# A fused tokeniser, attention and FFN kernel: a new order of all engines, queries placed by a maximum over one value, a buffer of its own for normalised rows

## The chip, the cores and the metric

One core of a Trainium2 chip. The metric is the device time of one execution in microseconds, as a median over executions. A profile of one further execution is shown, with its own time.

The engines are TensorE (PE; its weight loads have a row kind of their own, PEld), VectorE (DVE), ScalarE (ACT), GpSimd (POOL) and SyncE (SP), which in this kernel issues every DMA. Each engine runs its own instructions strictly in the order in which they were written; semaphores couple the engines. So an instruction that waits holds up everything behind it on its engine.

## The reference

64 images of 3 x 224 x 224 and 64 texts of 77 rows of 256 values. In essence:

```python
h = concat([tokens(x), txt], axis=1)              # 196 patch rows + 77 text rows, 256 wide
h = h + attention(layernorm(h))
h = h + ffn(layernorm(h))

def tokens(img):   # 14 x 14 patches of 768 values
    p = layernorm(patches(img)) * g + b
    return layernorm(p @ W + b) * g + b

def attention(x):  # per token: 16 heads attend to each other over the reshaped projections
    Q, K, V = proj(Wq, bq), proj(Wk, bk), proj(Wv, bv)
    return softmax(Q @ K.T * scale) @ V, then @ Wo.T + bo

def ffn(x):        # x_prev is x shifted by one token
    xr, xk = mu_r * x + (1 - mu_r) * x_prev, mu_k * x + (1 - mu_k) * x_prev
    return sigmoid(xr @ W_r) * (square(relu(xk @ W_k)) @ W_v)
```

By the labels of the reference's sums, for each token the 16 heads attend to one another (blocks of 16 by 16), and the result is reshaped without moving axes back, so that a row that goes into `Wo` holds one head's values of 16 tokens. The kernel therefore needs queries, keys and values in another layout than the projections give, and the attention's result in another again; both ways go through DRAM.

## The kernel before

Four images of 273 rows make a **quad** of 1092 rows, which is cut into three **chunks** of 364 rows (tiles of 126, 126 and 112 rows). There are 16 quads, 48 chunks, and the program is fully unrolled. While one chunk is in attention, the FFN of the chunk before and the tokeniser of images to come run between its steps, so that a chunk passes through several slots of the schedule.

The steps of a chunk that this text speaks of, with their lines:

- `qkv` (PE, L1048, output 126x384): projections, six products. `qb` (DVE, L863) adds the bias into `qkvt`.
- `qkv_out` (SP, L520): three DMAs, one for each tile, write `qkvt` to DRAM.
- `qk_in` (SP, L526): one DMA brings queries and keys back in the other layout, into `qk`. It waits for all three `qkv_out`.
- `qplace` (DVE, L849): two instructions put the queries into the two halves of the block-diagonal operand `qx`. `kspread` (ACT, L943): four instructions spread the keys. Both wait for `qk_in`.
- `s` (PE, L1085): scores, in two parts; waits for both `qplace` and all four `kspread`. Then `mx`, `sub` (DVE, L758, L763), `exp` (ACT, L948), `pt` (PE, L1093, transposes), `ptc` (ACT, L955).
- `v_in` (SP, L536): eight DMAs bring the values. `av` (PE, L1106): weighted values; waits for all eight `v_in`.
- `rec`, `osb` (DVE, L771, L775): normalise. `o_out` (SP, L541): nine DMAs to DRAM, once both `osb` are done. `o_in` (SP, L551): four DMAs bring the rows of an earlier chunk back as `on`, when the `o_out` that hold its last rows have landed.
- `ont` (PE, L1162), `onh`, `onl` (ACT, DVE): transposed rows; `wo` (PE, L1048, output 126x256), `h2` (DVE, L877): output projection and residual. `z` (ACT, L1005): normalised rows for the FFN, `zt` (PE, L1176) their transposes; `d`, `mix`, `k`, `r`, `val`, `add` the FFN; `out` (SP, L558) the result.
- Of images: `load` (SP, L489), `xcols`, `x`, `tok` (PE, L1116 and L1128), `h`, and `hdma` (SP, L513): three or four DMAs that put an image's finished patch rows into `hc`, the input rows of the chunks; `txt` (SP, L502) does the same for the text rows.

The order of every engine comes from one table of numbers, `AT`: each step has a position for each of its instructions, and every engine walks through all positions of a quad in rising order (`due`). A chunk step repeats every 4000 positions, an image step every 3000, a quad is 12000. A second table, `BANK`, gives each PE product its PSUM bank; `turn` makes PE wait for the last reader of what lay in that bank before.

One **slot** below is the stretch of 4000 positions in which one chunk goes from `o_out` of the chunk before it to its own `o_out`. The three slots of a quad differ in the image work that lies in them. In the order before, the first has `load` and `txt`, the second `load`, the third a whole `hdma` between `qkv_out` and `o_in`.

`on` and `z` are one buffer before: `o_in` waits until the transposes of the last `z` are through (L547), and `z` waits until `ont` has read `on` (L1003).

```python
def due(q, step, kind, j):
    k, rest = divmod(step - AT[kind][j], PERIOD[kind])
    if rest == 0 and exists(q, k, COUNT[kind]):
        yield k
```

Of the kernel before, what the change touches and what calls it, by code (L numbers as in the profile page):

```python
# [24 lines left out]
E = 256  # L25
HEADS, HD = 16, 16
# [5 lines left out]
TT = 126  # L32
TILES = 3
# [19 lines left out]
AT = dict(load=[0], xcols=[1555, 1687, 1876], sq=[3679], ssq=[4380], sqm=[4077, 4754], x=[2492, 2687, 2748],
    xh=[2643, 2784, 3076], xl=[2770, 3010, 3345], tok=[3700, 4609], stat=[4791], statc=[4894], statr=[4924],
    rstd1=[5338], txt=[10699], yn=[5350, 5424], st2=[6383, 6410], mv2=[6419, 6940], rstd2=[7253], hg=[6806, 7654],
    h=[7672, 8038], hdma=[9674], st3=[12693, 12843, 12966], mv3=[12988, 13082, 13112], rstd3=[13465], xn=[13777,
    13786, 13828], xt=[14114, 14194], xnh=[14323, 14438], xnl=[14474, 14695], hb=[18602], qkv=[14883, 15394, 15694,
    15965, 16265, 16340], qb=[15239, 15458, 15899, 16234, 16393, 16469], qkv_out=[16549, 17104, 17527],
    qk_in=[17953], v_in=[19005], qplace=[19042, 19048], kspread=[19082, 19222, 19230, 19256], s=[19435, 19452],
    mx=[19468, 19506], sub=[19575, 19604], exp=[19700, 19706], pt=[19710, 19922], ptc=[19888, 19894, 20053, 20060],  # L60
    av=[20075, 20094], rec=[20283, 20307], osb=[20293, 20332], o_out=[21113], o_in=[25935], ont=[26318, 26698],
    onh=[26409, 26726], onl=[26493, 26925], wo=[27035, 27261, 27330], h2=[27208, 27323, 27365], st4=[27324, 27769,
    27817], mv4=[27846, 27877, 27887], rstd4=[27943], z=[28233, 28349, 28364], zt=[28392, 28600], carry=[25727],
    ztc=[28522, 28666], d=[28888, 29076], edge=[29095], mix=[29171, 29248, 29941, 30014], mixh=[29528, 29665, 31342,
    31470], mixl=[29606, 29733, 31580, 31687], k=[30028, 30810], kr=[30222, 31508], ksq=[31257, 31771], kah=[31535,
    32120], kal=[31919, 32670], r=[32810, 33005, 33263], rt=[32874, 33121, 33343], val=[33333, 33595, 34000],
    rv=[33400, 33604, 34202], add=[34577, 35013, 35159], out=[34624, 36139, 37049], sqh=[4192])

BANK = dict(x=[5, 1, 3], tok=[1, 3], stat=[5], yn=[7], xt=[2, 4], qkv=[4, 5, 4, 6, 0, 2], s=[0, 6], pt=[2, 0],
    av=[2, 5], ont=[6, 0], wo=[5, 0, 6], zt=[4, 6], k=[5, 2], r=[0, 5, 2], val=[0, 2, 0])  # L70
BANK_ORDER = ("s", "pt", "av", "x", "tok", "stat", "xt", "qkv", "ont", "wo", "zt", "k", "r", "val", "yn")

XCUT = [(0, 5), (5, 10), (10, 14)]
# [1 line left out]
             "yn", "st2", "mv2", "rstd2", "hg", "h", "hdma")  # L75
PERIOD = {kind: IMG if kind in IMAGE_OPS else SLOT for kind in AT}
COUNT = {kind: IPQ if kind in IMAGE_OPS else CPQ for kind in AT}
STEPS = sorted({(a + PERIOD[kind] * i) % QUAD for kind, at in AT.items() for a in at for i in range(COUNT[kind])})
# [9 lines left out]
def exists(q, k, count):  # L88
    return not isinstance(q, int) or 0 <= count * q + k < count * QUADS
# [97 lines left out]
def fusion_kernel(nc, x, txt, ln1_g, ln1_b, tok_w, tok_b, ln2_g, ln2_b, wq, bq, wk, bk, wv, bv, wo, bo,  # L187
                  w_r, w_k, w_v, mu_r, mu_k, out):
    with ExitStack() as ctx:
        def sb(name, shape, dt=F32):  # L190
            return ctx.enter_context(nc.sbuf_tensor(name, shape, dt))

        def sig(name, per, primed=False, unit=1):
            return Signal(ctx, nc, name, per, CPQ, primed, unit)

        def isig(name, per, primed=False, unit=1):
            return Signal(ctx, nc, name, per, IPQ, primed, unit)
# [16 lines left out]
        xcols = sb("xcols", [XROWS, GRID * 128])  # L214
# [3 lines left out]
        rstd1 = sb("rstd1", [PT, 2])  # L218
# [4 lines left out]
        mv2 = sb("mv2", [PT, 2, 2])  # L223
# [12 lines left out]
        qx = sb("qx", [128, GR, 2, HD])  # L236
        qk = sb("qk", [128, GR, 2 * HD])
# [6 lines left out]
        osb = probs  # L244

        mx = sb("mx", [128, BLK // 4 * 8])
        rsum = mx
        pt2 = sb("pt2", [128, BLK, 2, 2, HD])


        on = sb("on", [TT, TILES, E])
        z = on
        onT = sb("onT", [128, 2, 2, CT], F32R)
        zT = sb("zT", [128, 2, 1 + CT])

# [1 line left out]
        kr = dT  # L257
# [3 lines left out]
        r = sb("r", [TT, TILES, E])  # L261
# [20 lines left out]
        def settle(eng):  # L282
            eng.sem_inc(settled, 1)
# [25 lines left out]
        st3 = sig("st3", 3)  # L309
# [30 lines left out]
        st4 = sig("st4", 3)  # L340
# [3 lines left out]
        z_pe = sig("z_pe", 2, True)  # L344
# [103 lines left out]
        def _(sp):  # L448
# [33 lines left out]
            def body(q):  # L482
                for s in STEPS:
# [59 lines left out]
                    for k in due(q, s, "o_in", 0):  # L543
                        after_all(o_out, q, k)
                        if k % CPQ < 2:
                            after_all(o_out, q, k + 1)
                        after(z_pe, q, k - 1, 2)  # L547
                        after(on_pe, q, k - 1, 2)
                        for m, r0, rows, i, p in row_pieces(k % CPQ):
                            src = o_dram[m, :, :, :].rearrange("q t d -> (q t d)").rearrange("(r e) -> r e", e=E)  # L550
                            on_in.done(sp.dma_start(on[p:p + rows, i, :], src[r0:r0 + rows, :]))  # L551
# [152 lines left out]
        def _(dve):  # L704
            V = nc.vector
# [41 lines left out]
            def body(q):  # L747
                for s in STEPS:
                    for n in weights_due(q, s):
                        square_weight(n)  # L750
                    for part in range(PARTS):
# [14 lines left out]
                        val, total = rows[:, :, 0:4 * HD].rearrange("p t (y d) -> p t y d", y=4), rows[:, :, 4 * HD:AVW]  # L766
# [76 lines left out]
                    for xx in range(2):  # L843
                        for k in due(q, s, "qplace", xx):
                            qk_in.wait(dve, q, k, 1)
                            s_pe.wait(dve, q, k - 1, PARTS)
                            settle(dve)
                            half = slice(64 * xx, 64 * xx + 64)
                            q_sb.done(V.tensor_copy(qx[half, :, xx, :], qk[half, :, 0:HD]))  # L849
                    for kk in range(2):  # L850
                        for k in due(q, s, "xnl", kk):
                            xn_hi.wait(dve, q, k, kk + 1)
# [53 lines left out]
        def _(act):  # L906
# [27 lines left out]
            def body(q):  # L934
                for s in STEPS:
# [64 lines left out]
                    for i, (o, rows) in enumerate(TOK):  # L1000
                        for k in due(q, s, "z", i):
                            rs4_pool.wait(act, q, k, 4)
                            on_pe.wait(act, q, k, 2)  # L1003
                            z_pe.wait(act, q, k - 1, 2)
                            z_sb.done(A.activation(z[0:rows, i, :], h2[0:rows, k % CPQ, i, :], ACT.Identity,  # L1005
                                                   bias=nm4[0:rows, i:i + 1], scale=rs4[0:rows, i:i + 1]))
# [212 lines left out]
```

How the kernel before makes its waits and increments, by code:

```python
    def wait(self, eng, q, k, steps):  # L162
        eng.wait_ge(self.sem, q * (self.count * self.per) + (self.base + k * self.per + steps * self.unit))
# [1 line left out]
    def done(self, ins):  # L165
        ins.then_inc(self.sem, self.unit)
        return ins
# [9 lines left out]
    def wait(self, eng, q, k):  # L177
        back, i = divmod(k, len(self.pers))
        eng.wait_ge(self.sems[i], q * self.pers[i] + (2 + back) * self.pers[i] + self.pers[i])
# [279 lines left out]
            def load_rest():  # L460
# [4 lines left out]
                        sp.dma_start(dst, v.rearrange("(a e) -> a e", a=1).broadcast_to((128, E))).then_inc(raw_in, 16)  # L465
                    for n, w in enumerate(WEIGHTS):
                        sp.dma_start(rawsq[n], w.rearrange("(a p) e -> p a e", p=128)).then_inc(raw_in, 16)
                    for s, v in ((0, mu_k), (1, mu_r)):
                        sp.dma_start(mus[:, s, :], v.rearrange("(k p) -> p k", p=128)).then_inc(raw_in, 16)
                sp.wait_ge(prep_pool, 1)
                for c in range(CPQ):
                    sp.dma_start(qkv_dram[c, CT:CTP, :, :].rearrange("t i j -> t (i j)"), qkvt[0:CTP - CT, 0, :]).then_inc(raw_in, 16)
# [9 lines left out]
            def body(q):  # L482
# [10 lines left out]
                    for k in due(q, s, "txt", 0):  # L493
                        back, m = divmod(k, IPQ)
                        c = back * CPQ + text_pieces(m)[-1][2]
                        if q * IPQ + k == 0:
                            sp.wait_ge(prep_act, ACT_CLEAR)
                        after(xn_sb, q, c - CPQ, 3)
                        after(hb_sb, q, c - CPQ, 1)
```

## Time and profile before

| what | value |
|---|---|
| median of 3 runs | 1629.72 us (1624.85 to 1634.03) |
| the profiled execution | 1621.5 us, span 1619.8 us |
| busy: PE, PEld | 1451.5 us (90%), 1383.3 us (85%) |
| busy: DVE, ACT, POOL | 1203.4 us (74%), 1107.2 us (68%), 1023.6 us (63%) |
| busy of the 16 DMA engines | 77.3% by the queue that SP issues on |
| granted PE clock, mean | 0.965 |

Busy times say what an engine had to do; whether it was waited for shows only in the views of waits and in the timeline. A row of the timeline is one or several instructions of a line that follow one another: start, length, engine and line, what is written from what, how many, and in brackets the idle time ahead of it with what ended it. A row of waits is engine and line, what it waited for, and then the sum, the count and the longest. SPq is SP's queue of instructions: the length of a DMA row there is how long SP took to issue it, not how long the transfer took.

### The profile page before, as it was taken

The page shows a single profiled execution, that of the slowest core. Times are in us where ns is not written, and L with a number is a line of the kernel's source. Part 1 is how long each engine was busy: PE and PEld are TensorE (multiplying, and loading weights), DVE is VectorE, ACT ScalarE, POOL GpSimd, SP SyncE. Part 2 cuts the span into 40 slices and gives each one's busy share as a digit, 9 for nine tenths or more (in the row PEclk, how much of TensorE's full clock was granted, in tenths as well). Part 3 has the DMA queues.
Part 4 walks back from the last instruction along what each step waited for, and adds up shares of the span by engine and source line. Part 5 has one row for each costly group of instructions (what it writes and reads, how often), then busy time and mean ns, then how long its engine had stood idle before and what let it go on. Part 6 is the DMA issues. An engine that isn't in the chain of part 4 may idle for free. (4 is left out here: it accounts for less than half of the span.)

```text
span 1619.8 us, 53760 instructions
## 1 busy us (share of the span) xinstructions
PE 1451.5 (90%) x18762; PEld 1383.3 (85%) x18762; DVE 1203.4 (74%) x3075; ACT 1107.2 (68%) x2230; POOL 1023.6 (63%) x1524
## 2 busy tenths in 40 slices
PE   4687899899989999999999999999999999988866
PEld 4677899798988989898999989998898889987756
DVE  5575787787867778787788868887778777877642
ACT  4554677677767777777777767777677677766643
POOL 3333567576666766766676766767676676666556
PEclk9798999999999999999999999999999999999988
DMA  5278889877977887797799788897888779778751
GB/s 137 53 144 137 129 157 147 135 149 154 159 132 150 143 148 159 160 148 163 136 151 162 145 151 137 171 161 136 158 148 150 144 151 154 152 132 130 132 79 38
DMA packets 702660, 227.67 MB, mean 141 GB/s; under 512 B 617470, under 2 KB 673854, under 8 KB 702394
## 3 DMA queue, kind: packets, MB, share of 16 engines
q1 hardware_dynamic: 702394, 224.23, 77.3%
q8 instruction: 153, 2.51, 0.7%
q14 instruction: 113, 0.93, 0.2%
HBM read 121.64 MB, written 89.64 MB: 130 GB/s over the span
## 5 line engine op out<-in xcount | busy, mean ns | idle before, releaser
L1048 PE MATMUL bank<-wqkv,xnT 128*126 128x384 f32 (+1 forms) x1728 | 359.1, 348 | 31.9 <-DVE h L877 22.9
L1048 PEld LDWEIGHTS bank<-wqkv,xnT 128*126 128x126 f32 (+1 forms) x1728 | 294.1, 185 | 44.0 <-issue 35.7
L1128 PE MATMUL bank<-wtok,xT 128*98 128x258 f32 x2304 | 314.9, 293 | 8.2 <-DVE xT L787 7.4
L1128 PEld LDWEIGHTS bank<-wtok,xT 128*98 128x98 f32 x2304 | 293.3, 172 | 11.2 <-DVE xT L787 8.5
L684 POOL TENSOR_TENSOR mixp<-mixf,mixp 128x364 fp32r<-128x364 f32 x192 | 183.6, 975 | 163.8 <-ACT mixp L1022 163.1
L943 ACT ACTIVATE arena<-qk,ymask 128x768 f32<-128x768 f32 x192 | 164.1, 930 | 72.9 <-DMA qk<-qkv_dram 72.9
L863 DVE TENSOR_TENSOR qkvt<-bank,bqkv 126x384 f32<-126x384 f32 (+1 forms) x288 | 156.0, 545 | 46.6 <-PE bank L1048 45.1
L632 POOL TENSOR_TENSOR xcols<-xcols 84x896 f32<-84x896 f32 x64 | 135.3, 2113 | 69.1 <-ACT xcols L977 68.3
L672 POOL TENSOR_TENSOR dT<-zT 128x364 f32<-128x364 f32 x96 | 75.2, 793 | 145.1 <-ACT zT L1016 144.9
L964 ACT ACTIVATE xcols<-xim 84x640 f32<-84x640 f32 (+1 forms) x192 | 129.6, 694 | 16.4 <-DVE xs L782 16.0
L621 POOL TENSOR_TENSOR rs<-ve,small 126x3 f32<-126x3 f32 (+1 forms) x160 | 129.2, 807 | 12.5
L972 ACT ACTIVATE xT<-bank 128x420 fp32r<-128x420 f32 (+1 forms) x192 | 101.1, 543 | 49.0 <-PE bank L1116 48.6
L894 DVE SCALAR_TENSOR_TENSOR mixf<-dT,mus,bank 128x364 f32<-128x364 f32 x192 | 105.8, 583 | 29.7 <-POOL dT L678 24.6
L1048 PE MATMUL bank<-wvfT,kaT 128*126 128x256 f32 (+1 forms) x864 | 126.0, 288 | 0.7 <-DVE r L900 0.7
L1048 PE MATMUL bank<-mixp,wkfT 128*128 128x364 f32 x576 | 119.5, 344 | 6.5 <-POOL mixp L684 5.7
L1048 PE MATMUL bank<-wrT,mixp 128*126 128x256 f32 (+1 forms) x864 | 118.5, 292 | 3.0 <-POOL mixp L684 2.4
L955 ACT ACTIVATE pt<-bank 64x384 f32<-64x384 f32 x192 | 93.1, 485 | 39.3 <-PE bank L1093 35.6
L787 DVE TENSOR_TENSOR xT<-bank,xT 128x420 fp32r<-128x420 f32 (+1 forms) x192 | 106.4, 557 | 15.3 <-ACT xT L972 15.1
L1016 ACT ACTIVATE zT<-bank 128x364 f32<-128x364 f32 x96 | 43.5, 473 | 108.5 <-PE bank L1176 108.1
L849 DVE COPY qx<-qk 64x768 f32<-64x768 f32 x96 | 69.5, 724 | 59.2 <-DMA qk<-qkv_dram 57.6
L1048 PEld LDWEIGHTS bank<-wrT,mixp 128*126 128x126 f32 (+1 forms) x864 | 110.0, 191 | 3.6 <-POOL mixp L684 2.7
L1048 PEld LDWEIGHTS bank<-wvfT,kaT 128*126 128x126 f32 (+1 forms) x864 | 110.7, 184 | 2.6 <-issue 1.4
(122 smaller groups left out, 3320.3 us busy)
## 6 DMA issues: line engine op xcount, KB each, us to landing
xim<-in_x SPq DMA_DIRECT2D x128, 294.0 KB
qk<-qkv_dram SPq DMA_DIRECT2D x48, 768.0 KB, 7.6
qkv_dram<-qkvt SPq DMA_DIRECT2D x96, 378.0 KB
arena<-qkv_dram SPq DMA_DIRECT2D x384, 48.0 KB, 3.9
qkv_dram<-qkvt SPq DMA_DIRECT2D x48, 336.0 KB
o_dram<-probs SPq DMA_DIRECT2D x288, 48.0 KB, 1.9
out<-h SPq DMA_DIRECT2D x96, 126.0 KB
on<-o_dram SPq DMA_DIRECT2D x64, 126.0 KB
```

The source lines that it names most:

```text
L621: done.done(P.tensor_tensor(rs[:, :], ve[:, :], powt[0:part, 0:ve.shape[1]], ALU.pow))
L632: x_half.done(P.tensor_tensor(halves[:, 0, :, :], halves[:, 0, :, :], halves[:, 1, :, :], ALU.add))
L684: mix_lo.done(P.tensor_tensor(mixp[:, w, 1, kk, :], mixf[:, kk, :], mixp[:, w, 0, kk, :].bitcast(F32), ALU.subtract))
L787: x_lo.done(V.tensor_tensor(xT[:, 1, :, w0:w1], src, xT[:, 0, :, w0:w1].bitcast(F32), ALU.subtract))
L863: qkv_sb.done(V.tensor_tensor(qkvt[0:rows, i, NQ * half:NQ * half + NQ], place("qkv", job)[0:rows, 0:NQ], bqkv[0:rows, :, :].rearrange("p ...
L894: mix_sb.done(V.scalar_tensor_tensor(out=mixf[:, kk, :], in0=dT[:, kk, :], scalar=mus[:, w, kk:kk + 1], in1=place("zt", kk)[:, 0:CT], op0= ...
L943: kb_sb.done(A.activation(kb[:, :, yy, :], qk[:, :, HD:2 * HD], ACT.Copy, scale=ymask[:, yy:yy + 1]))
L955: pt_sb.done(A.activation(pt2[64 * rr:64 * rr + 64, PB * part:PB * part + PB, :, rr, :], place("pt", part)[64 * rr:64 * rr + 64, 0:32 * PB ...
L964: x_cols.done(A.activation(xcols[:, 128 * w0:128 * w1].rearrange("p (w r q) -> p w r q", r=HALF, q=PS), xim[:, :].rearrange("p (r w q) -> ...
L972: x_hi.done(A.activation(xT[:, 0, :, w0:w1], src, ACT.Copy))
L1048: ins = mm(psum, left(a, k), right(b, k), start=t == 0, stop=t == len(terms) - 1)
L1128: ins = mm(place("tok", c)[0:PT, 0:E + 2], xT[:, a, i0:i0 + GRID // 2, :].rearrange("p i w -> p (i w)"), wtok[:, b, ch, :], start=t == 0, ...
```

## The change

Three edits.

1. **Order.** All numbers of `AT` and of `BANK` are new, so all engines, SP among them, run in another order, with other banks.
2. **A buffer for `z`.** `z` is its own tile, and the two waits that came with the sharing go: `o_in` on `z_pe`, and `z` on `on_pe`.
3. **`qplace`.** The two copies become `tensor_reduce` with a maximum over an axis of length 1. The values are the same.

```diff
-AT = dict(load=[0], xcols=[1555, 1687, 1876], sq=[3679], ...
+AT = dict(load=[0], xcols=[1286, 1360, 1572], sq=[3289], ...
...
-BANK = dict(x=[5, 1, 3], tok=[1, 3], stat=[5], yn=[7], xt=[2, 4], qkv=[4, 5, 4, 6, 0, 2], s=[0, 6], pt=[2, 0],
+BANK = dict(x=[5, 3, 1], tok=[3, 1], stat=[5], yn=[7], xt=[6, 0], qkv=[0, 6, 0, 2, 0, 2], s=[2, 4], pt=[4, 6],
...
         on = sb("on", [TT, TILES, E])
-        z = on
+        z = sb("z", [TT, TILES, E])
...
-                        after(z_pe, q, k - 1, 2)
                         after(on_pe, q, k - 1, 2)
...
-                            q_sb.done(V.tensor_copy(qx[half, :, xx, :], qk[half, :, 0:HD]))
+                            q_sb.done(V.tensor_reduce(qx[half, :, xx, :], qk[half, :, 0:HD].unsqueeze(3), AX.X, ALU.max))
...
                             rs4_pool.wait(act, q, k, 4)
-                            on_pe.wait(act, q, k, 2)
                             z_pe.wait(act, q, k - 1, 2)
```

What the new numbers do to the order, at the three places that matter here. Lines after the change are one or two lower (L541 becomes L540, L849 becomes L848).

**SP, first slot**, from the last `o_in` or `qk_in` to `v_in` (`arena` is the buffer that holds the values) and what follows. Before:

```order
L551 DMA on<-o_dram 91x256
L526 DMA qk<-qkv_dram 128x48x32
L558 DMA out<-h 126x256
L489 DMA xim<-in_x 42x1792 x2
L536 DMA arena<-qkv_dram 16x48x16 x8
L513 DMA hc<-yh 70x256
L513 DMA hc<-yh 28x256
L513 DMA hc<-yh 84x256
L513 DMA hc<-yh 14x256
```

Now:

```order
L525 DMA qk<-qkv_dram 128x48x32
L501 DMA hc<-in_txt 77x256
L512 DMA hc<-yh 70x256
L512 DMA hc<-yh 28x256
L512 DMA hc<-yh 84x256
L512 DMA hc<-yh 14x256
L556 DMA out<-h 126x256
L488 DMA xim<-in_x 42x1792 x2
L535 DMA arena<-qkv_dram 16x48x16 x8
```

`txt` and the four DMAs of `hdma` stood elsewhere (`txt` ahead of `o_in`, `hdma` behind `v_in`); now both are issued between `qk_in` and `v_in`, with `out` and `load`.

**SP, third slot**, from the last `qkv_out` to `v_in`. Before:

```order
L520 DMA qkv_dram<-qkvt 112x768
L513 DMA hc<-yh 98x256
L513 DMA hc<-yh 28x256
L513 DMA hc<-yh 70x256
L551 DMA on<-o_dram 91x256
L551 DMA on<-o_dram 35x256
L551 DMA on<-o_dram 126x256
L551 DMA on<-o_dram 112x256
L526 DMA qk<-qkv_dram 128x48x32
L558 DMA out<-h 126x256
L502 DMA hc<-in_txt 56x256
L502 DMA hc<-in_txt 21x256
L536 DMA arena<-qkv_dram 16x48x16 x8
```

Now:

```order
L519 DMA qkv_dram<-qkvt 112x768
L549 DMA on<-o_dram 91x256
L549 DMA on<-o_dram 35x256
L549 DMA on<-o_dram 126x256
L549 DMA on<-o_dram 112x256
L525 DMA qk<-qkv_dram 128x48x32
L556 DMA out<-h 126x256
L501 DMA hc<-in_txt 21x256
L501 DMA hc<-in_txt 56x256
L512 DMA hc<-yh 91x256
L512 DMA hc<-yh 7x256
L512 DMA hc<-yh 98x256
L535 DMA arena<-qkv_dram 16x48x16 x8
```

The `hdma` of three DMAs ahead of `o_in` is gone from there; another `hdma` of three now stands between `qk_in` and `v_in`. In the second slot it is the other way round: there `hdma` (four DMAs) stood between `qk_in` and `v_in` and now stands between `qkv_out` and `o_in`.

**DVE, around `qplace`**, in a slot with work on `xT`. Before:

```order
L869 TENSOR_TENSOR onT<-bank,onT 128x364
L787 TENSOR_TENSOR xT<-bank,xT 128x84x5
L849 COPY qx<-qk 64x48x16 x2
L877 TENSOR_TENSOR h<-bank,hb 126x256
L863 TENSOR_TENSOR qkvt<-bank,bqkv 126x384
L877 TENSOR_TENSOR h<-bank,hb 126x256
L880 BN_STATS bn<-h 126x6
L787 TENSOR_TENSOR xT<-bank,xT 128x84x4
L877 TENSOR_TENSOR h<-bank,hb 112x256
```

Now:

```order
L785 TENSOR_TENSOR xT<-bank,xT 128x84x5
L848 TENSOR_REDUCE qx<-qk 64x48x16
L876 TENSOR_TENSOR h<-bank,hb 126x256 x2
L785 TENSOR_TENSOR xT<-bank,xT 128x84x5
L848 TENSOR_REDUCE qx<-qk 64x48x16
L862 TENSOR_TENSOR qkvt<-bank,bqkv 126x384
L876 TENSOR_TENSOR h<-bank,hb 112x256
```

Both copies stood ahead of the first `h2` (which writes `h` from the bank of `wo`); now two `h2` stand between the two, and in this slot an `xT` as well. On PE, the product `qkv` whose bank is that of the first `wo` followed all three `wo` before; now another `qkv` and the last `wo` lie between the first `wo` and it. Also on PE, both `ont` now come straight after the first of the two transposes `xt`, which before both stood ahead of `ont`.

## Rows read from the trace of the kernel before

**Rows 1.** Windows view, 200 to 1480 us: stretch, length, busy us (instructions), clock, DMA.

```profile
200.00:1480.00 1280.00, 1208.25 (x16115) 1157.46 (x16114) 1012.28 (x2619) 933.38 (x1893) 867.92 (x1279) 0.99 0.84 149
```

**Rows 2.** Waits of PE from 200 to 1480 us.

```profile
PE bank L1048 <- DVE h L877: 17.4, 15, 2.0
PE bank L1162 <- DMA on<-o_dram: 16.2, 17, 2.6
```

**Rows 3.** Timeline of SP, a first slot.

```profile
613.44 5.23 SPq L541 DMA_DIRECT2D o_dram<-probs  x9
...
622.82 0.39 SPq L526 DMA_DIRECT2D qk<-qkv_dram  x1
...
629.32 7.81 SPq L536 DMA_DIRECT2D arena<-qkv_dram  x8
```

**Rows 4.** Timeline of SP, the second slot after it.

```profile
645.26 4.08 SPq L541 DMA_DIRECT2D o_dram<-probs  x9
...
652.65 0.39 SPq L526 DMA_DIRECT2D qk<-qkv_dram  x1
...
659.69 3.40 SPq L513 DMA_DIRECT2D hc<-yh  x4
663.28 5.38 SPq L536 DMA_DIRECT2D arena<-qkv_dram  x8
```

**Rows 5.** Timeline of SP, the third slot after it.

```profile
674.63 4.87 SPq L541 DMA_DIRECT2D o_dram<-probs  x9
...
680.21 2.50 SPq L513 DMA_DIRECT2D hc<-yh  x3
...
685.47 0.39 SPq L526 DMA_DIRECT2D qk<-qkv_dram  x1
...
691.50 4.48 SPq L536 DMA_DIRECT2D arena<-qkv_dram  x8
```

**Rows 6.** Timeline of ACT in the second slot: the four `kspread`.

```profile
660.26 3.42 ACT L943 ACTIVATE arena<-qk,ymask 128x768 f32<-128x768 f32 x4 [1.47 <-DMA qk<-qkv_dram]
```

**Rows 7.** Timeline of PE: `av` of the three slots, and `s` of the third.

```profile
641.15 1.79 PE L1106 MATMUL bank<-arena,pt 128*32 128x68 f32 x96
...
671.74 1.68 PE L1106 MATMUL bank<-arena,pt 128*32 128x68 f32 x96 [0.95 <-ACT pt L955]
...
697.41 1.62 PE L1085 MATMUL bank<-arena,qx 128*32 128x64 f32 x96
...
702.93 2.08 PE L1106 MATMUL bank<-arena,pt 128*32 128x68 f32 x96
```

**Rows 8.** Waits of SP over the whole span: for `osb`, and for `z_pe`.

```profile
SPq L283 <- DVE probs L775: 77.6, 36, 9.4
...
SPq L283 <- PE bank L1176: 12.0, 1, 12.0
```

**Rows 9.** DMA view, the last two `v_in` of the second slot: KB, us to landing.

```profile
arena<-qkv_dram SPq DMA_DIRECT2D x2, 48.0 KB, 3.5
```

**Rows 10.** DMA view, the last two `v_in` of the third slot.

```profile
arena<-qkv_dram SPq DMA_DIRECT2D x2, 48.0 KB, 4.6
```

**Rows 11.** Groups of DVE by form: busy us, mean ns of one.

```profile
L849 DVE COPY qx<-qk 64x768 f32<-64x768 f32 x96 | 69.5, 724 | 59.2 <-DMA qk<-qkv_dram 57.6
L782 DVE TENSOR_REDUCE xs<-xcols 84x14 f32<-84x896 f32 x64 | 68.9, 1077 | 32.7 <-POOL xcols L632 32.7
```

**Rows 12.** Source view of L849: ns min/median/max, first and last start.

```profile
L849 DVE COPY qx<-qk x96: 541/557/2515, 100.7 to 1548.1; 64x768 f32<-64x768 f32 x96
```

**Rows 13.** Timeline of DVE in the first slot: `xT`, both copies of one chunk, the first `h2`.

```profile
630.46 0.58 DVE L787 TENSOR_TENSOR xT<-bank,xT 128x420 fp32r<-128x420 f32 x1
630.96 1.75 DVE L849 COPY qx<-qk 64x768 f32<-64x768 f32 x2
632.74 0.42 DVE L877 TENSOR_TENSOR h<-bank,hb 126x256 f32<-126x256 f32 x1
```

**Rows 14.** Timeline of POOL at the same time.

```profile
630.90 0.80 POOL L689 TENSOR_TENSOR dT<-dT 128x364 f32<-128x364 f32 x1
```

More of the change, by code:

```diff
@@ L52 @@
 SLOT, IMG, QUAD = 4000, 3000, 12000
[L53 to L67, printed above, removed]
@@ L69 @@
-BANK = dict(x=[5, 1, 3], tok=[1, 3], stat=[5], yn=[7], xt=[2, 4], qkv=[4, 5, 4, 6, 0, 2], s=[0, 6], pt=[2, 0],
-    av=[2, 5], ont=[6, 0], wo=[5, 0, 6], zt=[4, 6], k=[5, 2], r=[0, 5, 2], val=[0, 2, 0])
+AT = dict(load=[0], xcols=[1286, 1360, 1572], sq=[3289], ssq=[4033], sqm=[4154, 4522], x=[2233, 2262, 2325],
+    xh=[2346, 2509, 2855], xl=[2437, 2890, 3072], tok=[3483, 4281], stat=[4290], statc=[4342], statr=[4356],
+    rstd1=[4876], txt=[8203], yn=[5071, 5080], st2=[6096, 6614], mv2=[6412, 6745], rstd2=[7116], hg=[6689, 7135],
+    h=[7151, 7277], hdma=[8401], st3=[12212, 12374, 12755], mv3=[12779, 12881, 12893], rstd3=[13150], xn=[13428,
+    13605, 13663], xt=[13790, 14108], xnh=[14103, 14209], xnl=[14200, 14339], hb=[15380], qkv=[14837, 14929, 15308,
+    15625, 15962, 15965], qb=[14929, 15093, 15671, 15727, 16040, 16073], qkv_out=[15524, 17019, 17289],
+    qk_in=[17928], v_in=[19407], qplace=[18710, 18904], kspread=[18610, 18648, 18721, 18823], s=[18976, 19119],
+    mx=[19109, 19173], sub=[19193, 19208], exp=[19467, 19489], pt=[19492, 19585], ptc=[19622, 19691, 19718, 19722],
+    av=[19692, 19783], rec=[19729, 19843], osb=[19823, 19872], o_out=[21287], o_in=[25703], ont=[25824, 25848],
+    onh=[25980, 26179], onl=[26168, 26231], wo=[26599, 26759, 26889], h2=[26751, 26867, 26931], st4=[27289, 27297,
+    27355], mv4=[27483, 27496, 27591], rstd4=[27778], z=[27938, 27946, 27953], zt=[28011, 28082], carry=[27118],
+    ztc=[28060, 28229], d=[28266, 28362], edge=[28742], mix=[28894, 28919, 29680, 29788], mixh=[29091, 29254, 29711,
+    31008], mixl=[29260, 29474, 30682, 31486], k=[29687, 29913], kr=[29857, 30972], ksq=[31172, 31497], kah=[31206,
+    31847], kal=[31708, 31911], r=[32313, 32463, 32853], rt=[32529, 32890, 32963], val=[33078, 33316, 33437],
+    rv=[33165, 33606, 33775], add=[34429, 34606, 34925], out=[34967, 35584, 36135], sqh=[3887])
@@ L71 @@
+BANK = dict(x=[5, 3, 1], tok=[3, 1], stat=[5], yn=[7], xt=[6, 0], qkv=[0, 6, 0, 2, 0, 2], s=[2, 4], pt=[4, 6],
+    av=[4, 6], ont=[5, 2], wo=[6, 2, 5], zt=[6, 4], k=[0, 4], r=[0, 2, 5], val=[2, 0, 5])
 BANK_ORDER = ("s", "pt", "av", "x", "tok", "stat", "xt", "qkv", "ont", "wo", "zt", "k", "r", "val", "yn")
```

## The prediction

> **What bounds the kernel now.** I read the windows first. Between 200 and 1480 us PE is busy 1208.25 of 1280 us at a granted clock of 0.99 [rows 1]: at most 72 us can be had there. The waits of PE [rows 2] name what it stood for: `h2` ahead of a `qkv` whose bank is that of the first `wo` (17.4 us, 15 times), and the rows `on` from DRAM ahead of `ont` (16.2 us, 17 times). Both stand close ahead of the scores and hang on transfers, so I followed the chain of those on SP. A slot goes: `o_out`, then `o_in`, `qk_in`, `kspread`, `s`, `av`, `osb`, and the next `o_out`. It is closed: the next `o_out` needs this `av`.
>
> In three slots that follow one another, SP takes from the start of `o_out` to that of `qk_in` 9.4 us (613.44 to 622.82) [rows 3], 7.4 us (645.26 to 652.65) [rows 4] and 10.8 us (674.63 to 685.47) [rows 5]. The third is longest because `hdma` (2.50 us for three) stands there. In the second slot `kspread` begins 7.6 us after `qk_in`, straight on its landing, and takes 3.42 us [rows 6]. `av` starts 18.3, 19.1 and 17.5 us after its `qk_in` (at 641.15, 671.74 and 702.93) [rows 7]. From there to the next `o_out` are 4.1 us (641.15 to 645.26) and 2.9 us (671.74 to 674.63). With 2.9 for the third, the slots are 31.8, 29.4 and 31.2 us, 92.4 a quad, and 16 quads make 1478 of the span of 1619.8 us; the rest is filling and draining. So this chain sets the period, with PE close behind it: the reader is to watch what moves a step of the chain, not busy time.
>
> **The change, part by part.** Per quad, from these rows.
>
> *First slot, to `qk_in`.* `txt` leaves, but `o_in` waits for the landing of `o_out` anyway: -0.2 us (9.4 to 9.2).
>
> *Second slot, to `qk_in`.* Four `hdma` come in ahead of `o_in`, 3.40 us for four [rows 4]. The third slot, with three at 2.50, is 3.4 longer there than the second without: between 0 (hidden behind the landing of `o_out`) and +4.5 (3.4 x 4/3). The row of four itself is the nearest, less a little for that landing: +3.1. On the other side SP now comes late to this `o_out`, because `hdma` and `v_in` pile up ahead of it: 4.1 us after `av` in place of 2.9. SP waits for `osb` in only 36 of 48 chunks [rows 8], so in 12, one a quad, it is the late one. Now `hdma` no longer stands there: of the 1.2 us I take -0.8.
>
> *Third slot, to `qk_in`.* Three `hdma` leave: -2.50 by their row [rows 5], -3.4 by the difference to the second slot: I take -2.8.
>
> *`v_in` of the first slot.* It starts 6.5 us after `qk_in` now (629.32) [rows 3], and one `txt` and four `hdma` come ahead of it: five DMAs at 0.85 each, so 10.7. That is where the second slot's stands now (663.28, 10.6 after `qk_in`), whose issue ends at 668.66 [rows 4] and whose last two land 3.5 us after issue [rows 9], at about 671.7, 19.0 after `qk_in`. That is the very moment its `av` starts, after 0.95 us of idle PE [rows 7], which the view gives to `pt`. In the first slot `av` wants its values by 18.3 at the latest. Low bound 0 (they land as quickly as would just do); high bound +3.1 (issue takes 7.81 us as it does there now, landing at 21.4). I take +1.0, close to the second slot's landing, since its list of work is the same.
>
> *`v_in` of the second slot.* `hdma` goes from ahead of it, and the 0.95 us with it, which I count in about every second quad: -0.4.
>
> *`v_in` of the third slot.* It starts 6.0 us after `qk_in` (691.50), ends its issue at 695.98, and the last two land 4.6 us after theirs [rows 10], at about 700.3, 14.9 after `qk_in`. Three `hdma` now stand ahead: 2.7 later, 17.6. `av` starts at 17.5 in this instance, 5.5 after `s` (697.41) [rows 7]; but `s` began 11.9 after `qk_in`, where the second slot's `kspread` was through at 11.0 (663.68) in spite of a slow landing. So `av` may want its values at 16.6: +0.1 to +1.0; I take +0.7.
>
> *The maximum.* 96 copies cost 724 ns each now. A `tensor_reduce` of 84x896 takes 1077 ns [rows 11]; 768 of 896 of that are 0.92 us. Bounds: 0.56, the copy's median [rows 12], and 1.26, by the 0.42 us that `h2` takes for 256 outputs [rows 13], as no reduce here writes one output for each input. DVE works 96 x 0.2 = 19 us more; it is idle for a quarter of the span. `qplace` runs beside `kspread`, which takes 3.42 us from the same landing [rows 6]. With two `h2` between, both reduces are through after 0.92 + 0.84 + 0.92 = 2.7 us, with an `xT` (0.58) too after 3.3: the cost is 0. Without that cover it would be 0.4 us a chunk.
>
> One rule speaks for it, one against. The two copies of a pair took 1.75 us where two medians are 1.11 (630.96) [rows 13], while POOL had an instruction of 0.80 us (630.90) [rows 14]; the longest copy took 2515 ns [rows 12]. The Trainium skill, SBUF — State Buffer, section Who interferes with whom, says that a copy in a two-port mode and GpSimd lock each other out, and that `tensor_reduce` on trn2 never contends; this pair agrees. Against it the Trainium skill, VectorE: DVE Perf Modes, section Rules for kernel authors, calls `tensor_reduce` on a hot path the slowest DVE operation, to be expected at 1x. The rows agree there too: 1.2 ns an element for the reduce, 0.7 for the median copy. By the first alone DVE would gain some 16 us, by the second it would lose 35; neither is in the sum, as both lie beside `kspread`.
>
> *DVE and PE around `qkv`.* The wait for `h2` could go whole: 17.4 us in 13.8 quads are 1.3 each. But that `qkv` stands straight ahead of `s`, which waits for `kspread` as well, and `kspread` (3.42 us) outlasts the two copies and an `h2` (2.2 us) [rows 13]: what of the 1.3 is hidden there comes back as a wait of `s`. Bounds 0 and -1.3; I take -0.4. `ont` now comes half a transpose earlier, so where PE waits for `on` [rows 2] it waits 0.4 longer, about once a quad: +0.4.
>
> *`z`'s own buffer.* SP's wait on `z_pe` was the last one a single time, 12.0 us [rows 8], in the drain, where the same FFN steps are the work to be finished anyway; ACT's wait for `ont` comes three PE steps and a `wo` after it and is long past by then. 0. If an `o_in` did hang on it, the loss removed would be that one 12 us at most.
>
> **Sum per quad:** to `qk_in` -0.2 + 3.1 - 0.8 - 2.8 = -0.7; `v_in` +1.0 - 0.4 + 0.7 = +1.3; PE 0. Together +0.6 us. Over 15 quads of steady work +9 us. The sum is made against the profiled execution, 1621.5 us, which lies 8.2 us below the median of 1629.72; I carry the difference over to the median: **1639 us**, +0.6%. Filling and draining I leave as they are (within 5 us).
>
> **The rivals.**
>
> 1. *Values in time (faster).* Place: `v_in` of the first and third slots. If their issue, which then falls behind the landing of `qk_in`, is as quick as the third slot's now (4.48 us against 7.81), both land before `av` asks. Then the terms are -0.7 on SP, -0.4 on the second slot, -1.3 for `h2`, and 0.4 of it back: -2.0 a quad, -30 us, 1600 us. It decides at a landing 18 us after `qk_in` in the first slot. For it: SP's queue is freer there. Against: the second slot's row, which lands at 19.0 with the same work ahead.
> 2. *Values later still (slower).* `load` straight ahead of `v_in` keeps the issue at 7.81 us: +2.1 in the first slot and +0.3 in the third above my values. That makes the sum +3.0; since the issue is that long in some quads only, I take +2.4 for it, 36 us, 1666 us. The reduce at 1.26 us with `xT` in between (3.9 against 3.42, in one slot of three) would belong here too, +8 us by itself.
> 3. *Nothing moves.* PE takes over wherever the chain gives way (it is busy 94% of that window), and `v_in` just fits: 1630 us, the change not doing what its size suggests.
>
> **How the numbers follow.** About 0.5% (8 us) is what a measurement of this kernel can tell from no change. My forecast has 0.45 with a range of its own from 1624 to 1656, somewhat more of it above that bound: 0.26 slower, 0.19 no change. Rival 1 has 0.34, rival 2 0.14, rival 3 0.07. Faster 0.34, no change 0.26, slower 0.40. Eight in ten lie between 1598 and 1668.
>
> **What would show it.** In the profile after: `av` of the first and third slots idle, with `v_in` landing just ahead; nearly no wait for `h2`; `o_out` to `qk_in` about 9.2, 10.5 and 8.0 us; SP waiting for `osb` in nearly all chunks; L848 near 0.92 us with minimum and maximum close together. The period of three slots should be 93.0 us. I am wrong if it is below 92, if `av` never idles, or if `s` waits for `qplace`.

## The result, and the profile after

1675.29 us as a median of four executions (1672.11 to 1680.58), beside 1631.88 us for the kernel before (four, 1624.85 to 1634.19): **slower by 2.8%, ratio 1.0277 with an interval of 1.0234 to 1.032**. The ratio here, and in the table of experiments, is that of the means over executions in the faster of two states that the chip shows, so it differs a little from the quotient of the medians. The forecast was 1639 us (+0.6%); its own range ended at 1656, the one for eight in ten at 1668. The sign, to which the forecast had given 0.40, was right and the place was right; the size was not.

The same windows view (stretch, length, busy us of PE, PEld, DVE, ACT, POOL, clock, DMA share, GB/s) and the waits of PE in that stretch, after the change, and one line of PE's waits in that stretch from the kernel before:

```profile
200.00:1480.00 1280.00, 1180.65 (x15468) 1128.58 (x15457) 994.09 (x2520) 906.63 (x1828) 833.43 (x1235) 0.97 0.78 145
```

```profile
PE bank L1104 <- DMA arena<-qkv_dram: 37.6, 19, 4.2
PE bank L1160 <- DMA on<-o_dram: 14.8, 18, 2.8
PE bank L1046 <- DVE h L876: 11.1, 10, 2.6
...
PE bank L1083 <- DVE qx L848: 2.0, 3, 0.7
```

```profile
PE bank L1106 <- DMA arena<-qkv_dram: 0.3, 1, 0.3
```

PE is busy 1180.65 us where it was 1208.25 [rows 1], at nearly the same clock (0.97 for 0.99). What is new among its waits is the first line: `av` stood 37.6 us for the values, 19 times; before, that line (L1106 there) had 0.3 us. The waits for `on` and for `h2` went down a little (14.8 and 11.1 us for 16.2 and 17.4 [rows 2]). PE's matmuls of `s` stood 2.0 us for `qplace` there.

SP's timeline through three slots that follow one another, first, second and third:

```profile
527.36 4.47 SPq L540 DMA_DIRECT2D o_dram<-probs  x9
...
535.85 0.39 SPq L525 DMA_DIRECT2D qk<-qkv_dram  x1
536.42 4.44 SPq L501 DMA_DIRECT2D hc<-in_txt  x1
541.12 3.30 SPq L512 DMA_DIRECT2D hc<-yh  x4
...
545.13 0.78 SPq L488 DMA_DIRECT2D xim<-in_x  x2
546.09 7.83 SPq L535 DMA_DIRECT2D arena<-qkv_dram  x8
```

```profile
560.85 4.02 SPq L540 DMA_DIRECT2D o_dram<-probs  x9
...
565.59 3.07 SPq L512 DMA_DIRECT2D hc<-yh  x4
...
570.80 0.39 SPq L525 DMA_DIRECT2D qk<-qkv_dram  x1
571.31 6.73 SPq L488 DMA_DIRECT2D xim<-in_x  x2
...
578.75 7.94 SPq L535 DMA_DIRECT2D arena<-qkv_dram  x8
```

```profile
593.62 4.54 SPq L540 DMA_DIRECT2D o_dram<-probs  x9
...
602.60 0.39 SPq L525 DMA_DIRECT2D qk<-qkv_dram  x1
...
608.54 2.47 SPq L512 DMA_DIRECT2D hc<-yh  x3
611.20 5.65 SPq L535 DMA_DIRECT2D arena<-qkv_dram  x8
```

And `av` of these three slots on PE:

```profile
556.74 2.97 PE L1104 MATMUL bank<-arena,pt 128*32 128x68 f32 x96 [3.29 <-DMA arena<-qkv_dram]
...
590.17 1.87 PE L1104 MATMUL bank<-arena,pt 128*32 128x68 f32 x96
...
619.80 1.68 PE L1104 MATMUL bank<-arena,pt 128*32 128x68 f32 x96 [0.93 <-DMA arena<-qkv_dram]
```

The reader compares with [rows 3 to 5] and [rows 7]. In the first slot `v_in` starts 10.2 us after `qk_in` (535.85 to 546.09), close to the forecast 10.7; its issue then takes 7.83 us, and `av` starts at 20.9 after `qk_in`, having idled 3.29 us for the values. In the third slot it is 0.93 us. In the second, `o_out` to `qk_in` is 9.95 us with `hdma` in it, and `av` does not idle.

Over the 12 slots of each kind between 275 and 1435 us of each trace, the means are (us; from SP's, ACT's and PE's rows, as above):

| step | 1st before, after | 2nd before, after | 3rd before, after |
|---|---|---|---|
| last `osb` to `o_out` | 0.25, 0.17 | 0.94, 0.17 | 0.17, 0.72 |
| `o_out` to `qk_in` | 8.14, 8.52 | 8.74, 10.51 | 10.45, 8.35 |
| `qk_in` to its landing | 7.42, 7.46 | 8.09, 8.38 | 7.56, 7.24 |
| landing to `s` | 4.03, 3.95 | 3.79, 3.74 | 4.01, 3.95 |
| `s` to `av` | 7.21, **10.16** | 7.78, 7.62 | 5.67, **6.56** |
| `av` to last `osb` | 3.04, 3.46 | 2.74, 3.19 | 3.24, 2.83 |
| slot | 30.08, 33.73 | 32.08, 33.61 | 31.11, 29.66 |
| issue of the eight `v_in` | 7.77, 7.86 | 5.86, 7.44 | 4.75, 5.82 |

The three slots are 93.3 before and 97.0 after: 3.7 us a quad. Over 13 to 15 quads that is 48 to 56 us, beside 53.4 us between the two profiled spans (1619.8 and 1673.2) and 43.4 us between the medians.

The source view of the maximum (ns min/median/max), with what waited for it (us, times), and the same two lines for the copies before:

```profile
L848 DVE TENSOR_REDUCE qx<-qk x96: 932/948/952, 98.9 to 1603.7; 64x768 f32<-64x768 f32 x96
...
  PEld bank L1083: 27.2, 22
  PE bank L1083: 9.2, 5
```

```profile
  PEld bank L1085: 11.5, 3
  PE bank L1085: 5.7, 1
```

Its price came out as forecast, 0.95 us, and hardly varies, where the copy went up to 2515 ns [rows 12]. But over the whole span `s` (weight loads and matmuls) waited for `qplace` 27 times where it had waited 4 times. That is one of the three signs by which the prediction said it would be wrong. It did not lengthen the step: from the landing of `qk_in` to `s` the table has no slot that grew.

### The profile page after: what moved, and what is told of

Same layout as the page of the kernel before. It is cut to its first block and busy times, and to the rows that moved or that the text cites. A ratio compares the mean times of both kernels' runs of the same rounds, so it can differ in the third digit from the quotient of the medians.

```text
span 1673.2 us, 53712 instructions
## 1 busy us (share of the span) xinstructions
PE 1466.0 (88%) x18762; PEld 1393.6 (83%) x18762; DVE 1225.4 (73%) x3075; ACT 1113.0 (67%) x2230; POOL 1017.7 (61%) x1524
## 5 line engine op out<-in xcount | busy, mean ns | idle before, releaser
L1046 PE MATMUL bank<-wqkv,xnT 128*126 128x384 f32 (+1 forms) x1728 | 363.4, 351 | 21.8 <-DVE h L876 14.1
L658 POOL TENSOR_TENSOR hb<-hc,bob 126x768 f32<-126x768 f32 x48 | 88.2, 1837 | 123.5 <-DVE h L876 123.5
L1104 PEld LDWEIGHTS bank<-arena,pt 128*32 128x32 f32 x4608 | 87.3, 119 | 68.6 <-issue 48.3
L1104 PE MATMUL bank<-arena,pt 128*32 128x68 f32 x4608 | 97.2, 242 | 53.9 <-DMA arena<-qkv_dram 40.6
L848 DVE TENSOR_REDUCE qx<-qk 64x768 f32<-64x768 f32 x96 | 90.9, 947 | 61.2 <-DMA qk<-qkv_dram 59.5
L963 ACT ACTIVATE xcols<-xim 84x640 f32<-84x640 f32 (+1 forms) x192 | 126.7, 695 | 10.4 <-DVE xs L780 7.5
L1046 PE MATMUL bank<-wrT,mixp 128*126 128x256 f32 (+1 forms) x864 | 123.3, 292 | 3.3 <-POOL mixp L682 2.4
L1046 PE MATMUL bank<-wvfT,kaT 128*126 128x256 f32 (+1 forms) x864 | 122.5, 288 | 0.0
```

What stands on the lines that cost most here:

```text
L963: x_cols.done(A.activation(xcols[:, 128 * w0:128 * w1].rearrange("p (w r q) -> p w r q", r=HALF, q=PS), xim[:, :].rearrange("p (r w q) -> ...
L1046: ins = mm(psum, left(a, k), right(b, k), start=t == 0, stop=t == len(terms) - 1)
L1104: ins = mm(place("av", part)[32 * j:32 * j + 32, col:col + AVW], pt2[:, b, xx, :, :].rearrange("p r q -> p (r q)"), vrow[:, g, 0:AVW], sta ...
```

## The experiments

A run's ratio is to the kernel before on the same chip. In the edits, `SHIFT` is a small table that moves single occurrences of a step: the first number is the image or chunk within the quad, the second is added to its position; nothing but SP's order changes by it. The experiments ran on several chips, in groups. To set one ratio against that of another group, or against the 1.0277 of the result, supposes that a ratio carries over from chip to chip, which no run here shows.

| run | median, us | before, us | ratio (95% interval) |
|---|---|---|---|
| e1_values_first | 1650.42 | 1622.41 | 1.0193 (1.0148 to 1.0237) |
| e2_before_values_late | 1613.27 | 1622.41 | 0.9938 (0.9899 to 0.9978) |
| e3_load_behind_values | 1645.43 | 1622.41 | 1.0159 (1.0121 to 1.0198) |
| e4_copy_again | 1677.30 | 1622.41 | 1.0358 (1.0300 to 1.0416) |
| e5_hdma_out_of_second | 1688.66 | 1619.09 | 1.0440 (1.0383 to 1.0498) |
| e6_changed_sp_mended | 1653.98 | 1619.09 | 1.0232 (1.0183 to 1.0280) |
| e7_before_max_and_buffer | 1632.17 | 1619.09 | 1.0062 (1.0025 to 1.0100) |
| e8_before_sp_mended | 1770.24 | 1619.09 | 1.0933 (1.0874 to 1.0992) |
| e9_values_ahead_of_hdma | 1630.95 | 1619.63 | 1.0072 (1.0034 to 1.0110) |
| e10_hdma_behind_load | 1641.71 | 1619.63 | 1.0129 (1.0080 to 1.0178) |
| e11_both_moves | 1604.49 | 1619.63 | **0.9904** (0.9869 to 0.9939) |
| e12_both_moves_copy | 1603.34 | 1619.63 | **0.9883** (0.9834 to 0.9932) |
| e13_before_max_only | 1628.64 | 1622.64 | 1.0034 (1.0000 to 1.0068) |
| e14_before_buffer_only | 1610.44 | 1622.64 | 0.9962 (0.9924 to 1.0000) |

### Is it the values, and why so late?

**The changed kernel, values first.**

```diff
-v_in=[19407]
+v_in=[17930]
```

> The changed kernel with `v_in` straight behind `qk_in` on SP (one number of the table). Theory A (the values come late): the waits of `av` for the values go in the first slot (about 2.3 to 3.0 us) and in the third (about 1.0), together 3.3 to 4 us a quad, some 15 quads: 1615 to 1627 us, back at the kernel before or below it. Theory B (the maximum makes the scores wait): `s` still waits for `qplace`, 1665 to 1676 us. Theory C (the four `hdma` ahead of `o_in` in the second slot, +1.8 us a quad): 1650 us or more, since they stay there.

The ratio fell from 1.0277 to 1.0193, not to 1. The waits of `av` for the values went, although the issue of `v_in`, now straight behind the 768 KB of `qk_in`, takes 9.6 to 10.0 us: first slot 30.8 us for 33.7, third 28.3 for 29.7. But the second grew from 33.6 to 36.4. Waits of ACT, and of PE from 200 to 1480 us, in this run:

```profile
ACT xcols L963 <- DMA xim<-in_x: 58.5, 15, 5.0
```

```profile
PE bank L1091 <- ACT probs L947: 17.8, 11, 2.2
```

With the values first, `load` is issued behind them; ACT waits for the loaded image 58.5 us (1.2 in the changed kernel), and the exponentials, queued behind that step on ACT, hold up `pt` (17.8 us; no such line in that stretch of the changed kernel). One late transfer was traded for another.

**The changed kernel, only `load` and `v_in` of the first slot exchanged.**

```diff
+SHIFT = {"load": {1: 410}}
```

> The changed kernel with only the `load` of the first slot moved from just ahead of `v_in` to just behind it. A2: the issue of the eight `v_in` falls from 7.9 to about 5.9 us, and with the issue of `load` itself the values land 2.5 to 3 us earlier: 1633 to 1645 us. A1: the issue stays long, only the 0.9 us of `load` itself is won: 1658 to 1666 us. B and C: 1670 us or more.

The ratio is 1.2 of the 2.8 points lower; times the 1631.88 us of the result it is 1658 us, at the lower edge of A1's range. By the issue A2 held. SP's timeline in a first slot, and PE's wait:

```profile
530.10 0.59 SPq L531 DMA_DIRECT2D qk<-qkv_dram  x1
...
535.75 3.29 SPq L518 DMA_DIRECT2D hc<-yh  x4
539.23 0.41 SPq L562 DMA_DIRECT2D out<-h  x1
539.82 6.06 SPq L541 DMA_DIRECT2D arena<-qkv_dram  x8
546.34 0.77 SPq L494 DMA_DIRECT2D xim<-in_x  x2
```

```profile
PE bank L1110 <- DMA arena<-qkv_dram: 11.6, 13, 2.1
```

The same eight `v_in`, behind the same four `hdma`, are issued in 6.06 us here; over 12 slots 5.70 in place of 7.86, and they land 18.35 us after `qk_in` in place of 20.92. SP is through with them 3.0 us earlier: 0.9 of that is the issue of `load`, which no longer stands ahead, and 2.2 the shorter issue of `v_in`. Of the 37.6 us for which `av` waited, 11.6 are left.

**The kernel before, `v_in` of the first slot behind its `hdma`.**

```diff
-v_in=[19005]
+v_in=[19680]
```

> The kernel before with `v_in` of the first slot put behind that slot's four `hdma`, nothing else moved: `load`, four `hdma`, `v_in`. Theory A1 (the four DMAs ahead shift the values by their 3.5 us, to 21 us after `qk_in`, where `av` asks at 18.5): +2.4 a quad, 1663 to 1671 us. Theory A2 (`load` straight ahead of `v_in` is what makes its issue 7.9 us long; with `hdma` between, it takes 5.9 and lands at 18.9): +0.5 a quad, 1634 to 1643 us. Theories B and C: no change, 1625 to 1635 us.

Both sizes were wrong: it is 0.6% faster. SP in a first slot, and SP's wait for `osb`:

```profile
516.07 0.39 SPq L526 DMA_DIRECT2D qk<-qkv_dram  x1
...
521.52 0.76 SPq L489 DMA_DIRECT2D xim<-in_x  x2
522.88 4.00 SPq L513 DMA_DIRECT2D hc<-yh  x4
527.07 5.98 SPq L536 DMA_DIRECT2D arena<-qkv_dram  x8
```

```profile
SPq L283 <- DVE probs L775: 95.9, 46, 8.8
```

A2's part held: with `hdma` between `load` and the values, their issue takes 5.67 us over 12 slots where it took 7.77, and they land only 1.2 us later (18.66 for 17.49 after `qk_in`), which costs `av` 0.5. What neither theory had is that SP, its long issue shortened, is in time for the next `o_out`: it waits for `osb` 46 times of 48 in place of 36 [rows 8], and the second slot is 30.85 us for 32.08. The forecast put SP's lateness in the kernel before down to `hdma` and `v_in` together. All twelve DMAs still stand ahead of that `o_out` here, and SP is no longer late: what made it late was the long issue of `v_in` straight behind `load`.

### The second slot's `hdma`

**The changed kernel, these four behind `v_in`.**

```diff
+SHIFT = {"hdma": {3: 2100}}
```

> The changed kernel with the four `hdma` of the second slot moved from ahead of `o_in` to behind that slot's `v_in`; everything else as changed, so the values of the first and third slots stay late. Theory C (these four are worth 1.8 us a quad by the traces of before and after, 3.1 by the forecast): 1648 us by the first, 1630 by the second. If the chain does not set the period where PE is close behind: 1665 us or more.

Slower still. `qk_in` did start 2.8 us earlier (7.73 us after `o_out`), but `s` to `av` rose from 7.62 to 11.11. Waits of the whole span:

```profile
DVE yh L830 <- DMA hc<-yh: 63.2, 15, 6.2
...
PE bank L1097 <- ACT probs L953: 45.8, 18, 5.2
```

`hdma` reads `yh`, and the next image writes it on DVE, in this order in the middle of the softmax. That write now waited 63.2 us for `hdma`, and the exponentials with it (PE stood 45.8 us for them, 3.0 in the changed kernel). The step has a deadline of its own: the next write to `yh`.

**The changed kernel with three moves.**

```diff
+SHIFT = {"v_in": {2: -1106, 1: -106}, "hdma": {3: 2100}}
```

> The changed kernel with three moves on SP: `v_in` ahead of `hdma` in the first slot (behind `txt`) and in the third (behind `txt`), and the four `hdma` of the second slot behind its `v_in`; `load` stays ahead of `v_in` in the second slot, where the run with the values first in all slots had ScalarE wait for the loaded image with the exponentials queued behind. If SP's order is the whole of the loss: first slot -2.7, second -1.8, third -0.9, together some 5 us a quad, 1600 us, below the kernel before. If the new order of the other engines, the maximum or the buffer costs something as well, it stays above 1622 us.

The first and third slots came to 30.9 and 28.1 us as expected; the second to 35.9, for the same wait for `yh`. So the move of the values works, and that of the second slot's `hdma` to behind `v_in` does not.

**The kernel before, third slot's `hdma` behind `v_in`.**

```diff
-v_in=[19005]
+v_in=[19680]
+SHIFT = {"hdma": {0: 2080}}
```

> The kernel before with two moves on SP: `v_in` of the first slot behind its four `hdma` (as in the run that was faster), and the three `hdma` of the third slot moved from ahead of `o_in` to behind `v_in`. If the chain sets the period: another 2.4 us a quad off, 36 us below the run with the first move, some 1580 us. If PE takes over (72 us idle of 1280, some 30 of it instruction fetch): 1595 us or so.

9% slower, for the same reason: waits of the whole span, and of PE from 200 to 1480 us.

```profile
DVE yh L832 <- DMA hc<-yh: 161.1, 15, 13.3
```

```profile
PE bank L1054 <- DVE xnT L859: 120.7, 13, 10.4
```

The wait for `yh` holds up `xnT` behind it on DVE, and so all of PE. The `hdma` ahead of `o_in` in the kernel before, which the forecast counted as pure delay of the chain (-2.8 us when it goes), has to be done before the next write to `yh`, some 1000 positions behind it in that kernel's table.

**The changed kernel, `hdma` of the second slot behind `load`,** late enough to leave the chain, early enough for `yh`.

```diff
+SHIFT = {"hdma": {3: 609}}
```

> The changed kernel with the four `hdma` of the second slot moved from ahead of `o_in` to behind `load`, still ahead of the next image's `yh` on VectorE, which the run with them behind `v_in` missed. `qk_in` of that slot then starts some 2.5 us earlier, `v_in` 3.5 later but without `load` straight ahead: -1.5 to -2 us a quad, 1645 to 1655 us. If `yh` waits again: 1675 us or more.

The second slot fell from 33.61 to 30.41 us; 1.5 points of 2.8.

**The changed kernel, `v_in` ahead of `hdma` in the first and third slots.**

```diff
+SHIFT = {"v_in": {2: -1106, 1: -106}}
```

> The changed kernel with `v_in` of the first and third slots moved from behind `hdma` (and, in the first, `load`) to straight behind `txt`; the second slot as changed, with its four `hdma` ahead of `o_in`. Late values are the loss: first slot -2.9, third -0.9 to -1.5, together about 4 us a quad, 60 us: 1610 to 1622 us. If waits that they hid come up in their place, 1640 us or more.

Two points of the 2.8 went: first slot 30.78, third 28.57 us, the second unchanged at 34.00.

**Both moves.**

```diff
+SHIFT = {"v_in": {2: -1106, 1: -106}, "hdma": {3: 609}}
```

> Both moves together: values ahead of `hdma` in the first and third slots, `hdma` behind `load` in the second. If SP's order is the whole of the loss: first slot 30.9, second 31.6, third 28.1 us, 90.6 a quad against 93.3 of the kernel before: 1575 to 1595 us, faster than before by 2 to 3%. If the rest of the new order costs something, 1610 us or more.

1604 us, below the kernel before by 1% (1.3 to 0.6%), though by less than expected. Windows and waits of PE:

```profile
200.00:1480.00 1280.00, 1219.41 (x16311) 1164.97 (x16312) 1044.18 (x2639) 950.58 (x1915) 873.33 (x1297) 0.99 0.84 151
```

```profile
PE bank L1166 <- DMA on<-o_dram: 14.3, 13, 2.8
PE bank L1052 <- DVE h L882: 11.4, 15, 1.6
...
PE bank L1089 <- DVE qx L854: 7.1, 11, 0.7
...
PE bank L1110 <- DMA arena<-qkv_dram: 0.8, 2, 0.5
```

SP in a second slot, from its `o_out` to `v_in`:

```profile
540.70 4.83 SPq L546 DMA_DIRECT2D o_dram<-probs  x9
...
548.75 0.39 SPq L531 DMA_DIRECT2D qk<-qkv_dram  x1
549.26 6.21 SPq L494 DMA_DIRECT2D xim<-in_x  x2
555.72 3.06 SPq L518 DMA_DIRECT2D hc<-yh  x4
...
559.51 5.59 SPq L541 DMA_DIRECT2D arena<-qkv_dram  x8
```

Of the wait of `av` for the values 0.8 us are left, in two waits; `s` now stands 7.1 us for `qplace`, which had been 2.0. What the sum of slots had missed is SP again: the `o_out` that opens the third slot now starts 1.63 us after its `osb` is ready, with `txt`, `hdma` and `load` ahead of it. So with these few DMAs moved the new order is 1% faster than the kernel before as it stands. That is not to say that the other engines' order is better: the kernel before, with its own `v_in` moved (e2), is at 0.9938 (0.9899 to 0.9978), and the two intervals overlap.

### The maximum and the buffer

**The changed kernel with the copies.**

```diff
-q_sb.done(V.tensor_reduce(qx[half, :, xx, :], qk[half, :, 0:HD].unsqueeze(3), AX.X, ALU.max))
+q_sb.done(V.tensor_copy(qx[half, :, xx, :], qk[half, :, 0:HD]))
```

> The changed kernel with the two copies back in place of the maximum. Theory A: `av` waits for the values just as long whether `s` starts 0.3 us earlier or not, 1670 to 1676 us. Theory B: the 36 us in which `s` waited for `qplace` go, 1640 to 1650 us. The copies' mean should go up from the median of 0.56 again where POOL works beside them.

Theory B fell: ratio 1.0358, nothing won. The test is narrower than it was meant to be: with the copies `s` waited for `qplace` 24 times, 38.0 us, where it was 27 times and 36.4 us with the maximum. So the wait belongs to the new order and not to the instruction, and no run moves `qplace` alone. **Both moves, with the copies:**

> As the run with both moves, with the two copies in place of the maximum. Where the values are no longer late, what `qplace` costs can show: `s` waited for it in 27 of 96 parts in the changed kernel, 36 us in all, most of it beside `kspread`. If the maximum costs on the path: 8 to 15 us faster than with it. If the copies lose as much beside POOL: the same within 5 us.

0.9883 (0.9834 to 0.9932) against 0.9904 (0.9869 to 0.9939): the same. **The kernel before with both edits,** with the maximum alone, and with the buffer alone:

> The kernel before with the maximum in place of the copies and with the buffer of its own for `z` without its two waits, tables unchanged: edits 2 and 3 alone. By the forecast (both cost nothing, 0 within 8 us): 1614 to 1631 us. With both reduces ahead of the first `h2` (1.9 us in place of 1.1 to 1.75), `qkv` behind `h2` may come 0.2 to 0.8 us later than `kspread` allows: up to +10 us at most.

> The kernel before with the maximum in place of the copies, alone. Theory M (in the order before, both reduces stand ahead of the `h2` that a `qkv` ahead of `s` waits for: 1.9 us of them in place of 1.1 to 1.75): slower by 0.3 to 0.9%, as much as with both edits. Theory Z (the buffer costs): no change, within 0.3%.

> The kernel before with a buffer of its own for `z` and without the two waits, alone. Theory M: no change, within 0.3%. Theory Z (where tiles lie in memory, or which work runs early, changes and costs): slower by 0.3 to 0.9%.

+0.6% together, +0.3% and -0.4% alone, the last two with intervals that end at no change. Each alone is measured at under half a per cent, with intervals that reach 0.7 and 0.8; that together they come to more than their sum (0 or so) is within what these intervals leave, and stays open.

## Why the prediction was wrong in size

Step by step, forecast and measured (us a quad, from the table of slots):

- **`v_in` of the first slot: +1.0, measured +2.95.** This is the step that failed. The forecast had the row that says so: in the first slot, with `load` straight ahead, the issue takes 7.81 us [rows 3]. I took the second slot's 5.38 [rows 4] instead, "since its list of work is the same". The list is the same but for `txt`, and its order is not: there `hdma` stands between `load` and `v_in`. So the landing was put at 19.0 us after `qk_in` and came at 20.9, close to the 21.4 of the high bound; 1.95 of the 3.1 us a quad by which the sum fell short are this term. Exchanging `load` and `v_in` gave 1.2 of the 2.8 points back, and the rival that had exactly this (7.81 us kept, 1666 us) was given 0.14. Where two rows could price a step, the one with the same neighbour straight ahead was the right one. That the start of `v_in` came out (10.7 forecast, 10.4 measured) is partly luck: `txt`, priced at 0.85 us, took 4.5 us straight behind `qk_in`; in its place went a wait of about as long that the forecast had carried over, SP's for the rows of `out`, 4.6 us in the slot of [rows 3].
- `v_in` of the third slot: +0.7, measured +0.9. Of the second: -0.4, measured -0.2.
- Second slot to `qk_in`: +3.1, measured +1.8. SP in time for its `o_out`: -0.8, measured -0.8. Third slot to `qk_in`: -2.8, measured -2.1; but SP came late to that `o_out`, +0.55, with `txt`, `hdma` and `load` now ahead of it, for which the forecast had no term. First slot to `qk_in`: -0.2, measured +0.4.
- In sum over three slots: `s` to `av` +3.7 (forecast +1.3), last `osb` to `qk_in` -0.25 (forecast -0.7), landing to `s` -0.2, `av` to the last `osb` +0.5, for which the forecast had no step and the runs show no cause. That is the 3.7.
- The maximum: forecast 0.92 us and no cost on the path, measured 0.95 us and none that the runs show in the changed order. The buffer: forecast 0, measured between -0.8% and 0 alone.
- The wait for `h2` fell by 6.3 us and the wait for `on` by 1.4, of 17.4 and 16.2; beside 37 us of new waiting that is small. (The forecast had `on` going up by 0.4 us a quad and "nearly no wait" left for `h2`; 11.1 us were left.)
- The two moves on SP, 2.0 and 1.5 points of a loss of 2.8, together took the kernel 1% below before. So SP's order at these places is more than the whole loss. Whether the rest of the new order gains anything stays open, since the kernel before gained 0.6% by a move on SP as well.

Of the three signs of being wrong, a period below 92 us and an `av` that never idles did not come (97.0 us; 37.6 us of idling). The third, `s` waiting for `qplace`, did come, 27 times, but it is not what made the kernel slower: with both moves `s` still waits for it, and the kernel is 1% faster than before. Of what was to be seen, "`o_out` to `qk_in` about 9.2, 10.5 and 8.0", was 8.5, 10.5 and 8.35. "SP waiting for `osb` in nearly all chunks" was wrong: it was 38 of 48.

```profile
SPq L282 <- DVE probs L773: 103.1, 38, 8.8
```

## What to carry to other kernels

On a queue that one engine issues alone, price a moved transfer by its place. In these runs what stood just ahead of the eight `v_in` decided whether their issue took 5.5 or 8 us, and a step that was put earlier made what stood behind it later. Before moving a transfer out of a chain, look up both of its deadlines: who reads what it brings, and who waits to overwrite what it reads. And where the trace has the very instruction in the very place, its row goes before a row of the same instruction elsewhere.

## What the runs showed of the hardware

- Eight DMAs of 48 KB each, issued straight behind a `load` of two times 294 KB, took 7.8 to 7.9 us of SP's time (means over 12 slots of the kernel before and the changed one). With the four small DMAs of `hdma` between, it was 5.4 to 5.9 in four kernels (before, e2, e10, e11); with `load` behind them, 5.7 (e3). One `out` between was not enough: 7.4 in the changed kernel's second slot. Straight behind `qk_in`, one DMA of 768 KB, it was 9.6 to 10.0 (e1). It is the issue that is longer, not the way of the last transfer: in the first slot the eighth landed 3.2 us after the start of its issue in the changed kernel, and 3.9 with `load` behind. Why SP is held is not shown.
- A `tensor_reduce` over one value took 932 to 952 ns for 768 outputs in 64 rows in the changed kernel (910 to 953 in e7, with the order before); a copy of the same took 541 to 2515 ns in the kernel before, and with the copies put back into the changed kernel:

```profile
L848 DVE COPY qx<-qk x96: 532/558/1583, 102.2 to 1616.9; 64x768 f32<-64x768 f32 x96
```

The copy's median is the shorter one and its longest are longer. Of the copies before, 28 took more than 650 ns, and each of these ended 0.41 to 0.42 us after the end of an instruction of POOL that ran beside it. Of the 96 reduces after, 51 had an instruction of POOL beside them, and none took longer than 952 ns. That agrees with what the Trainium skill says in SBUF — State Buffer, section Who interferes with whom.
